# Normalising the residual sum of the MLP stage on ScalarE, with scale and bias per row from GpSimd, where VectorE subtracted and multiplied

## The chip, the cores and the metric

The kernel runs on one core of a Trainium2 chip. A core has TensorE (matmuls, PE in the profile; its weight loads are PEld), VectorE (DVE), ScalarE (ACT), GpSimd (POOL) and SyncE (SP), which here only issues transfers. The engines run side by side and are ordered by semaphores alone. The metric is the time of one execution on the device in microseconds; lower is better.

## The reference

The input `x` is 4096 tokens by 256. Three blocks follow each other, each with its own layernorm and residual sum:

```
x = x + 0.5 * ffn(layernorm(x))      # mixture of 8 experts (2 chosen) and a shared one
x = x + attn(layernorm(x))           # attention block with its own MLP, below
x = x + 0.5 * ffn(layernorm(x))

# inside attn, with z its input:
h = att @ Wo + bo + z
y = (h - mean(h)) * rsqrt(var(h) + 1e-5) * lnm_s + lnm_b
out = gelu(y @ W1 + b1) @ W2 + b2 + h
```

The change is in the line of `y`: the part `(h - mean) * rsqrt(var + eps)`. The factors `lnm_s` and `lnm_b` are folded into `W1` and `b1` when the stage starts.

## The kernel before

The program has four stages: `ffn_phase` (its names begin with `f_`), `attention_phase` (`a_`), `mlp_phase` (`m_`) and `ffn_phase` again (`g_`). Only `mlp_phase` is touched. It walks over the 4096 tokens in NB = 8 steps of 512, each held as NT = 4 tiles of 128 tokens by 256. Fp32 matmuls are made of three with split operands: for each operand ScalarE writes a rounded "hi" copy and VectorE the "lo" rest (`att_hi`/`att_lo`, `hT_hi`/`hT_lo`, `hid_hi`/`hid_lo`).

No scheduler sets the order. Each engine has a `body(i, par)`, written out by hand, and runs it for i = 0 to 8; steps 1 to 4 are turns of a loop. The order in one step i is:

- **TensorE**: first half of the projection of step i+1 (L1733), the second MLP matmul of step i-1 (`acc`, L1765), the transposes of `hn` (L1776, these wait for `hn` of step i), the second half of the projection of i+1, and the first MLP matmul (`hid`, L1789, which waits for `hT_lo`).
- **ScalarE**: four gelus and four `hid_hi` of step i-1, the first half of `att_hi` for step i+2 (L1561), two `hT_hi` (L1583), the second half of `att_hi`.
- **VectorE**: `h` (L1688), its statistics (L1691, L1696; mean and variance stand in `mv`), four `hid_lo` of step i-1 (L1658), the four rows of `hn` (L1707), the first half of `att_lo` for i+2 (L1653), two `hT_lo` (L1715), the second half of `att_lo`, and the result of step i-1 (L1724).
- **GpSimd**: `x_bias`, the second bias added to the residual input `xin` (four rows, L1621; it waits for the load of `xin`), then `rs = (var + eps)^-0.5` (L1638, L1640), then `xin += h` (L1643), then `z_bias` for step i+1, the first bias added to `zin` (four rows, L1621).
- **SyncE**: loads `zin` of i+1, two halves of the attention output of i+3 (L1504, each waits for the `att_lo` that frees its buffer), stores the result of i-1 (L1544, waits for L1724) and only then loads `xin` of i+1 (L1548).

So GpSimd's `rs`, and with it `hn`, stand behind the load of `xin`, and this load stands on SyncE's queue behind two halves of `att_lo` and the result of VectorE in the step before.

Of the kernel before, what the change touches and what calls it, by code (L numbers as in the profile page):

```python
# [23 lines left out]
ALU = mybir.AluOpType  # L24
ACT = mybir.ActivationFunctionType
AX = mybir.AxisListType

P = 128
# [7 lines left out]
DC = D // P  # L36
BT = 512
NT = BT // P
# [7 lines left out]
def stand_alone(eng, turns):  # L46


    eng.sem_inc(turns, 1)
# [1381 lines left out]
def mlp_phase(nc, turns, tag, w, att, z, x1, x2):  # L1431
# [9 lines left out]
    with ExitStack() as ctx:  # L1441
        m = Bank(nc, ctx, tag)
# [12 lines left out]
        mhalf = m.sb("mhalf", [P, NT])  # L1455
# [5 lines left out]
        h = m.sb("h", [P, NT, D])  # L1461
        st6 = m.sb("st6", [P, NT, 6])
        mv = m.sb("mv", [P, NT, 2])
        rs = m.sb("rs", [P, NT])
        hn = m.sb("hn", [P, NT, D])
        hT = m.sb("hT", [P, DC, 2, BT], F32R)
        act_out = m.sb("act_out", [P, HC, BT])
        hid_s = m.sb("hid_s", [P, HC, 2, BT], F32R)
        res = m.sb("res", [P, NT, D])
        proj = m.ps("proj", [P, NT, D])  # L1470
        hT_ps = m.ps("hT_ps", [P, DC, BT])
        hid = m.ps("hid", [P, 2, BT])
        acc = m.ps("acc", [P, NT, D])

        s = {n: m.sem(n) for n in (
            "w_in mhalf w1_scaled w_hi w_ready b1_ps att_in0 att_in1 att_hi att_lo z_in x_in zb x_b proj h bn stats "
            "veps rstd hn hT_ps hT_hi hT_lo hid gelu hid_hi hid_lo acc x_h res res_out").split()}
        NW = 8
        block = ctx.enter_context(nc.Block())

# [9 lines left out]
        def has(i, ahead=0):  # L1490

            return not isinstance(i, int) or 0 <= i + ahead < NB
# [59 lines left out]
        @block.scalar  # L1552
        def _(act):
            act.preload_act_table(ACT.Gelu_apprx_tanh)

            def att_hi(i, par, half):
                act.wait_ge(s["att_in%d" % half], i * 16 + 16)
                if has(i, -2):

                    act.wait_ge(s["proj"], i - 1)  # L1560
                act.activation(att_s[:, par, 0, half * HP:(half + 1) * HP], att_in[:, half],  # L1561
                               ACT.Identity).then_inc(s["att_hi"], 1)

            def gelu(i, hc):

                act.wait_ge(s["hid"], i * HC + hc + 1)
                act.activation(act_out[:, hc], hid[:, hc % 2], ACT.Gelu_apprx_tanh,
                               bias=b1[:, hc:hc + 1]).then_inc(s["gelu"], 1)

            def hid_hi(i, hc):  # L1570
                act.wait_ge(s["gelu"], i * HC + hc + 1)
                if has(i, -1):

                    act.wait_ge(s["acc"], i)
                act.activation(hid_s[:, hc, 0], act_out[:, hc], ACT.Identity).then_inc(s["hid_hi"], 1)

            def hT_hi(i):
                for c in range(DC):
                    act.wait_ge(s["hT_ps"], i * DC + c + 1)
                    if c == 0 and has(i, -1):  # L1580

                        act.wait_ge(s["hid"], i * HC)
                    act.activation(hT[:, c, 0], hT_ps[:, c], ACT.Identity).then_inc(s["hT_hi"], 1)  # L1583

            act.wait_ge(s["att_in0"], 16)
            act.activation(att_s[:, 0, 0, 0:HP], att_in[:, 0], ACT.Identity).then_inc(s["att_hi"], 1)
            act.wait_ge(s["att_in1"], 16)
            act.activation(att_s[:, 0, 0, HP:PAIRS], att_in[:, 1], ACT.Identity).then_inc(s["att_hi"], 1)
            act.wait_ge(s["w_in"], 16 * NW)
            act.activation(wo[:, 0], wo_in[:], ACT.Identity).then_inc(s["w_hi"], 1)  # L1590
            act.activation(w2[:, 0], w2_in[:], ACT.Identity).then_inc(s["w_hi"], 1)
            act.wait_ge(s["w1_scaled"], 1)
            act.activation(w1[:, 0], w1_in[:], ACT.Identity).then_inc(s["w_hi"], 1)
            for half in range(2):
                att_hi(1, 1, half)
            act.wait_ge(s["w_ready"], 3)

            def body(i, par):
                if has(i, -1):
                    gelu(i - 1, 0)  # L1600
                    for hc in range(1, HC):
                        gelu(i - 1, hc)
                        hid_hi(i - 1, hc - 1)
                    hid_hi(i - 1, HC - 1)
                if has(i, 2):
                    att_hi(i + 2, par, 0)
                if has(i):
                    hT_hi(i)
                if has(i, 2):
                    att_hi(i + 2, par, 1)  # L1610
            over_steps(act, body)

        @block.gpsimd
        def _(pool):
            pool.memset(mhalf[:], -0.5).then_inc(s["mhalf"], 1)
            pool.wait_ge(s["mhalf"], 1)
            pool.wait_ge(s["w_in"], 16 * NW)

            def add_rows(x, row):
                for t in range(NT):  # L1620
                    o = pool.tensor_tensor(x[:, t], x[:, t], row[:], ALU.add)  # L1621
                return o

            def z_bias(i, par):
                pool.wait_ge(s["z_in"], i * 16 + 16)
                add_rows(zin[:, par], bo).then_inc(s["zb"], 1)

            def x_bias(i, par):
                pool.wait_ge(s["x_in"], i * 16 + 16)
                add_rows(xin[:, par], b2).then_inc(s["x_b"], 1)  # L1630
            z_bias(0, 0)

            def body(i, par):
                if has(i):
                    x_bias(i, par)
                    pool.wait_ge(s["stats"], i + 1)
                    stand_alone(pool, turns)
                    pool.tensor_scalar(rs[:], mv[:, :, 1], EPS, None, ALU.add).then_inc(s["veps"], 1)  # L1638
                    pool.wait_ge(s["veps"], i + 1)
                    pool.tensor_tensor(rs[:], rs[:], mhalf[:], ALU.pow).then_inc(s["rstd"], 1)  # L1640

                    pool.wait_ge(s["x_b"], i + 1)
                    pool.tensor_tensor(xin[:, par], xin[:, par], h[:], ALU.add).then_inc(s["x_h"], 1)  # L1643
                if has(i, 1):
                    z_bias(i + 1, 1 - par)
            over_steps(pool, body)

        @block.vector
        def _(dve):
# [21 lines left out]
            for c in range(DC):  # L1671
                o = dve.tensor_scalar(w1_in[:, c], w1_in[:, c], ln[:, c, 0:1], None, ALU.mult)
# [8 lines left out]
            def body(i, par):  # L1681
                if has(i):
# [7 lines left out]
                    for t in range(NT):  # L1690
                        o = dve.bn_stats(st6[:, t], h[:, t])  # L1691
# [6 lines left out]
                if has(i, -1):  # L1698
                    for hc in range(HC):
                        hid_lo(i - 1, hc)  # L1700
                if has(i):
                    dve.wait_ge(s["rstd"], i + 1)
                    if has(i, -1):

                        dve.wait_ge(s["hT_ps"], i * DC)
                    for t in range(NT):
                        o = dve.tensor_scalar(hn[:, t], h[:, t], mv[:, t, 0:1], rs[:, t:t + 1],  # L1707
                                              ALU.subtract, ALU.mult)
                    o.then_inc(s["hn"], 1)
                if has(i, 2):  # L1710
                    att_lo(i + 2, par, 0)
                if has(i):
# [149 lines left out]
```

## Time and profile before

| | us |
|---|---|
| median of 3 runs | 2539.2 (2539.13 to 2540.71) |
| the profiled execution, whole | 2539.88 |
| its span in the profile | 2537.9 |
| busy PE / DVE / ACT / POOL | 2427.8 / 1911.5 / 1673.3 / 1496.3 |

The profile is of one execution. The rows of the trace give start and duration, in microseconds from the start of the span; the profiled execution is 1.98 us longer than its span. A row with `x4` merges four neighbouring instructions of a kind. The brackets at a row's end say how long the engine had been idle before it and what ended that. Ends of matmuls are modelled, so intervals between starts are safer on TensorE. The MLP stage takes its rows between about 2016 us, where its first loads are issued, and 2248 us.

### The profile page before, as it was taken

How to read it: one execution, taken by the hardware profiler on the slowest of the kernel's cores; microseconds unless marked ns; L12 is line 12 of the kernel's file. 1: busy time of each engine (PE TensorE's matmuls, PEld its weight loads, DVE VectorE, ACT ScalarE, POOL GpSimd, SP SyncE). 2: the span in 40 equal slices, each digit the busy share in tenths (PEclk: the TensorE clock that was granted, in tenths of full speed). 3: DMA queues.
4: the chain of work that ended last, by engine and by line, in shares of the span. 5: the costliest groups of instructions: out<-in, count | busy, mean ns of one | idle time of the engine just before them, and what ended most of it. 6: DMA issues, size and time to landing. Idle time of an engine off the chain costs nothing. (4 is left out here: it accounts for less than half of the span.)

```text
span 2537.9 us, 46611 instructions
## 1 busy us (share of the span) xinstructions
PE 2427.8 (96%) x14544; PEld 2107.4 (83%) x14544; DVE 1911.5 (75%) x3637; ACT 1673.3 (66%) x2887; POOL 1496.3 (59%) x1519
## 2 busy tenths in 40 slices
PE   7999899999999999999999999999999689959999
PEld 7888778888888888888888888888888589848888
DVE  4777677878878788787887878878788676736665
ACT  2455577878878777787877878878778533323333
POOL 2233377787677876878768777777776344412221
PEclk9999999999999999999999999999999899969999
DMA  3322531222212222122221222212221244321111
GB/s 131 142 99 91 176 115 42 84 77 81 92 42 83 80 77 92 42 83 83 75 91 42 83 83 75 91 42 88 78 75 51 87 164 153 100 89 34 50 50 42
DMA packets 128666, 212.73 MB, mean 84 GB/s; under 512 B 7652, under 2 KB 90776, under 8 KB 119960
## 3 DMA queue, kind: packets, MB, share of 16 engines
q1 hardware_dynamic: 128536, 211.36, 25.8%
q14 instruction: 93, 0.76, 0.1%
q8 instruction: 37, 0.61, 0.1%
HBM read 112.77 MB, written 48.23 MB: 63 GB/s over the span
## 5 line engine op out<-in xcount | busy, mean ns | idle before, releaser
L1295 DVE TENSOR_REDUCE a_nmax<-a_sc 128x1 f32<-128x1024 f32 x512 | 626.8, 1224 | 256.6 <-PE a_sc L1374 248.4
L1223 POOL TENSOR_SCALAR a_pr<-a_pr,a_rden 128x1024 f32<-128x1024 f32 x512 | 576.2, 1126 | 274.3 <-DVE a_rden L1300 204.0
L1147 ACT ACTIVATE a_pT<-a_tr 128x512 fp32r<-128x512 f32 x1024 | 559.9, 596 | 209.4 <-PE a_tr L1386 203.4
L1306 DVE TENSOR_TENSOR a_pT<-a_tr,a_pT 128x512 fp32r<-128x512 f32 x1024 | 650.4, 677 | 16.3 <-ACT a_pT L1147 16.3
L1410 PE MATMUL a_ov<-a_pT,a_v_s 128*128 128x512 f32 x2048 | 598.8, 414 | 2.4 <-DVE a_half L1286 1.4
L1153 ACT ACTIVATE a_pr<-a_sc,a_nmax 128x1024 f32<-128x1024 f32 x512 | 573.9, 1121 | 32.9 <-DVE a_nmax L1295 29.5
L1374 PE MATMUL a_sc<-a_k_s,a_q_s 128*128 128x512 f32 x2048 | 555.0, 393 | 8.1 <-DMA a_k_s<-a_k_s 7.8
L1386 PEld LDWEIGHTS a_tr<-f_ident,a_pr 128*128 128x128 f32 x4096 | 473.9, 140 | 91.5 <-DVE a_pT L1306 18.4
L1386 PE MATMUL a_tr<-f_ident,a_pr 128*128 128x128 f32 x4096 | 537.7, 273 | 8.6 <-DVE a_pT L1306 8.5
L1374 PEld LDWEIGHTS a_sc<-a_k_s,a_q_s 128*128 128x128 f32 x2048 | 380.9, 188 | 89.4 <-DMA a_k_s<-a_k_s 8.0
L1410 PEld LDWEIGHTS a_ov<-a_pT,a_v_s 128*128 128x128 f32 x2048 | 346.3, 189 | 53.2 <-issue 4.9
L1329 PE MATMUL a_pj<-a_z_s,a_wqk_s 128*128 128x512 f32 x756 | 193.8, 391 | 0.4 <-issue 0.4
L1329 PEld LDWEIGHTS a_pj<-a_z_s,a_wqk_s 128*128 128x128 f32 x756 | 141.7, 188 | 32.8 <-issue 0.8
L405 ACT ACTIVATE g_act_out<-g_hid,g_b 128x512 f32<-128x512 f32 x72 | 49.6, 688 | 154.2 <-PE g_hid L748 154.2
L1116 ACT ACTIVATE a_staged<-a_pj,f_bias 128x512 f32<-128x512 f32 x126 | 86.8, 689 | 88.7 <-PE a_pj L1329 66.4
L405 ACT ACTIVATE f_act_out<-f_hid,f_b 128x512 f32<-128x512 f32 x72 | 49.2, 684 | 118.3 <-PE f_hid L748 118.3
L782 PEld LDWEIGHTS f_acc<-f_w2p,f_hp 128*128 128x128 f32 x864 | 112.2, 190 | 9.3 <-DVE f_hp L591 4.5
L782 PEld LDWEIGHTS g_acc<-g_w2p,g_hp 128*128 128x128 f32 x864 | 112.5, 191 | 7.6 <-DVE g_hp L591 2.3
L782 PE MATMUL f_acc<-f_w2p,f_hp 128*128 128x256 f32 x864 | 115.9, 284 | 2.4 <-DVE f_hp L591 1.8
L748 PE MATMUL g_hid<-g_xT,g_w1p 128*128 128x512 f32 x432 | 116.9, 407 | 1.2 <-DVE g_w1p L643 1.2
L782 PE MATMUL g_acc<-g_w2p,g_hp 128*128 128x256 f32 x864 | 115.8, 284 | 0.9 <-DVE g_hp L591 0.4
L748 PE MATMUL f_hid<-f_xT,f_w1p 128*128 128x512 f32 x432 | 115.5, 403 | 0.0
(221 smaller groups left out, 3216.6 us busy)
## 6 DMA issues: line engine op xcount, KB each, us to landing
a_z_s<-zT SPq DMA_DIRECT2D x32, 1024.0 KB, 7.4
a_k_s<-a_k_s SPq DMA_DIRECT2D x64, 512.0 KB, 5.6
a_wqk_s<-w_split SPq DMA_DIRECT2D x64, 256.0 KB, 3.1
a_v_s<-a_v_b SPq DMA_DIRECT2D x16, 1024.0 KB, 4.6
att<-a_ao SPq DMA_DIRECT2D x32, 512.0 KB, 2.9
m_att_in<-att SPq DMA_DIRECT2D x16, 1024.0 KB, 5.4
a_wv_s<-w_split SPq DMA_DIRECT2D x17, 512.0 KB, 3.8
zT<-f_zT SPq DMA_DIRECT2D x8, 1024.0 KB, 3.9
```

The source lines that it names most:

```text
L405: act.activation(act_out[:, e % 3], hid[:, (par + e) % 2], ACT.Gelu, bias=b1[:, weights_of(e):weights_of(e) + 1]).then_inc(s["gelu"], 1)
L748: o = pe.matmul(hid[:, (par + e) % 2], w1p[:, a, (c * NE + x) * HID:(c * NE + x + 1) * HID], xT[:, par, c, b], start=(n == 0), stop=(n == 5))
L782: o = pe.matmul(acc[:, t], hp[:, e % 3, a, t * P:(t + 1) * P], w2p[:, b, x * D:(x + 1) * D], start=False, stop=(e == NE - 1 and (a, b) == ...
L1147: act.activation(pT[:, (u // 4) % 2, 0, 4 * part:4 * part + 4, (u % 4) * P:(u % 4 + 1) * P], tr[:, part].rearrange("p (t q) -> p t q", t=4 ...
L1153: act.activation(pr[:, k % NP], sc[:, k % 2], ACT.Exp, bias=nmax[:, k % NP:k % NP + 1], accum_out=den[:, k % NP:k % NP + 1]).then_inc(s["e ...
L1223: pool.tensor_scalar(pr[:, k % NP], pr[:, k % NP], rden[:, k % NP:k % NP + 1], 1.0, ALU.mult, ALU.mult).then_inc(s["normed"], 1)
L1295: dve.tensor_reduce(nmax[:, k % NP:k % NP + 1], sc[:, k % 2], AX.X, ALU.max, negate=True).then_inc(s["negmax"], 1)
L1306: dve.tensor_tensor(to[:, 1], tr[:, part].rearrange("p (t q) -> p t q", t=4), to[:, 0].bitcast(F32), ALU.subtract).then_inc(s["tr_lo"], 1)
L1329: o = pe.matmul(bank[:], wqk_s[:, "QK".index(kind), c, a], z_s[:, c * 2 + b, part], start=(i == 0), stop=(i == 5))
L1374: o = pe.matmul(sc[:, k % 2, kb * BT:(kb + 1) * BT], q_s[:, slot, head, tile * P:(tile + 1) * P], k_s[:, slot, head, a, kb * BT:(kb + 1) * ...
L1386: o = pe.transpose(tr[:, part, j * P:(j + 1) * P], pr[:, (k - LAG) % NP, (4 * part + j) * P:(4 * part + j + 1) * P], ident[:])
L1410: o = pe.matmul(ov[:], v_s[:, vslot, kt, 2 * vhead:2 * vhead + 2] .rearrange("p k f -> p (k f)"), pT[:, blk % 2, a, kt], start=(kt == 0 an ...
```

## The change

ScalarE works out `hn = h * rs + shift` with `rs` as scale and `shift = -mean * rs` as bias, both one value for each partition. GpSimd works out `shift` in two more instructions of 128x4: `-mean` ahead of the `rs` steps, and the product behind the power. The signal on which `hn` waits (`rstd`) now comes from the product; the power signals `powed`. ScalarE does `hn` behind the `hid_hi` of step i-1 and ahead of the first half of `att_hi`. VectorE's four instructions go.

```
@@ ScalarE, body(i, par)
                     hid_hi(i - 1, HC - 1)
+                if has(i):
+                    act.wait_ge(s["rstd"], i + 1)
+                    if has(i, -1):
+                        act.wait_ge(s["hT_ps"], i * DC)
+                    for t in range(NT):
+                        o = act.activation(hn[:, t], h[:, t], ACT.Identity, bias=shift[:, t:t + 1], scale=rs[:, t:t + 1])
+                    o.then_inc(s["hn"], 1)
                 if has(i, 2):
                     att_hi(i + 2, par, 0)
@@ GpSimd, body(i, par)
                     pool.wait_ge(s["stats"], i + 1)
+                    if has(i, -1):
+                        pool.wait_ge(s["hn"], i)
                     stand_alone(pool, turns)
+                    pool.tensor_scalar(shift[:], mv[:, :, 0], -1.0, 0.0, ALU.mult, ALU.add)
                     pool.tensor_scalar(rs[:], mv[:, :, 1], EPS, None, ALU.add).then_inc(s["veps"], 1)
                     pool.wait_ge(s["veps"], i + 1)
-                    pool.tensor_tensor(rs[:], rs[:], mhalf[:], ALU.pow).then_inc(s["rstd"], 1)
+                    pool.tensor_tensor(rs[:], rs[:], mhalf[:], ALU.pow).then_inc(s["powed"], 1)
+                    pool.wait_ge(s["powed"], i + 1)
+                    pool.tensor_tensor(shift[:], shift[:], rs[:], ALU.mult).then_inc(s["rstd"], 1)
@@ VectorE, body(i, par)
-                if has(i):
-                    dve.wait_ge(s["rstd"], i + 1)
-                    if has(i, -1):
-                        dve.wait_ge(s["hT_ps"], i * DC)
-                    for t in range(NT):
-                        o = dve.tensor_scalar(hn[:, t], h[:, t], mv[:, t, 0:1], rs[:, t:t + 1],
-                                              ALU.subtract, ALU.mult)
-                    o.then_inc(s["hn"], 1)
                 if has(i, 2):
                     att_lo(i + 2, par, 0)
```

ScalarE's order in a turn of the loop, before, from the last `hid_hi` on (`m_att_s` is written by `att_hi`, `m_hT` by `hT_hi`):

```order
L1575 ACTIVATE m_hid_s<-m_act_out 128x512 x2
L1557 ISA
L1561 ACTIVATE m_att_s<-m_att_in 128x2048
L1579 ISA
L1582 REGISTER_ALU
L1583 ACTIVATE m_hT<-m_hT_ps 128x512
```

The same place of ScalarE's order after the change (`m_hn` is the normalised sum, `m_shift` and `m_rs` its bias and scale):

```order
L1576 ACTIVATE m_hid_s<-m_act_out 128x512 x2
L1610 REGISTER_ALU
L1612 ACTIVATE m_hn<-m_h,m_shift,m_rs 128x256 x4
L1558 ISA
L1562 ACTIVATE m_att_s<-m_att_in 128x2048
L1580 REGISTER_ALU
```

The four rows of `hn` now stand ahead of the first half of `att_hi`, which used to run while ScalarE had nothing else to do.

GpSimd's order in a turn of the loop, before:

```order
L1621 TENSOR_TENSOR m_xin<-m_xin,m_b 128x256 x4
L1636 REGISTER_ALU
L1638 TENSOR_SCALAR m_rs<-m_mv 128x4
L1640 TENSOR_TENSOR m_rs<-m_rs,m_mhalf 128x4
L1643 TENSOR_TENSOR m_xin<-m_xin,m_h 128x1024
```

GpSimd's order at this place after the change:

```order
L1630 TENSOR_TENSOR m_xin<-m_xin,m_b 128x256 x4
L1645 REGISTER_ALU
L1649 TENSOR_SCALAR m_shift<-m_mv 128x4
L1650 TENSOR_SCALAR m_rs<-m_mv 128x4
L1652 TENSOR_TENSOR m_rs<-m_rs,m_mhalf 128x4
L1654 TENSOR_TENSOR m_shift<-m_shift,m_rs 128x4
L1657 TENSOR_TENSOR m_xin<-m_xin,m_h 128x1024
```

Two small instructions are added, one ahead of the old pair and one behind it; the large sum `xin += h` and `z_bias` follow as before.

## Rows read from the trace of the kernel before

**Rows 1.** Busy time by stage (us from:to, length, engines, clock, DMA).

```profile
2052.00:2217.00 165.00, 160.41 (x1184) 151.49 (x1184) 119.15 (x158) 61.11 (x79) 67.59 (x77) 1.00 0.40 129
```

**Rows 2.** TensorE's waits in the MLP stage: us in total, times, longest.

```profile
PE m_acc L1765 <- DVE m_hid_s L1658: 5.2, 2, 2.6
PE m_hT_ps L1776 <- DVE m_hn L1707: 3.6, 5, 2.2
```

**Rows 3.** TensorE in order of time (start, us), steps 0, 1, 2 and 5.

```profile
2052.95 5.93 PE L1733 MATMUL m_proj<-m_wo,m_att_s 128*128 128x256 f32 x48 [1.41 <-DVE m_h L1688]
2061.10 1.09 PE L1776 MATMUL m_hT_ps<-m_ident,m_hn 128*128 128x128 f32 x8 [2.21 <-DVE m_hn L1707]
...
2079.00 5.84 PE L1765 MATMUL m_acc<-m_w,m_hid_s 128*128 128x256 f32 x48
2084.68 1.03 PE L1776 MATMUL m_hT_ps<-m_ident,m_hn 128*128 128x128 f32 x8
...
2102.59 5.84 PE L1765 MATMUL m_acc<-m_w,m_hid_s 128*128 128x256 f32 x48
2108.75 1.09 PE L1776 MATMUL m_hT_ps<-m_ident,m_hn 128*128 128x128 f32 x8 [0.32 <-DVE m_hn L1707]
...
2181.11 1.09 PE L1776 MATMUL m_hT_ps<-m_ident,m_hn 128*128 128x128 f32 x8 [0.33 <-DVE m_hn L1707]
```

**Rows 4.** All other engines in step 2, from one `xin` load to the next.

```profile
2092.48 0.43 SPq L1548 DMA_DIRECT2D m_xin<-x  x1
...
2099.80 2.81 POOL L1621 TENSOR_TENSOR m_xin<-m_xin,m_b 128x256 f32<-128x256 f32 x4 [15.49 <-DMA m_xin<-x]
...
2102.58 0.23 POOL L1638 TENSOR_SCALAR m_rs<-m_mv 128x4 f32<-128x4 f32 x1
...
2103.90 2.40 POOL L1643 TENSOR_TENSOR m_xin<-m_xin,m_h 128x1024 f32<-128x1024 f32 x1
2104.06 4.63 DVE L1707 TENSOR_SCALAR m_hn<-m_h,m_mv,m_rs 128x256 f32<-128x256 f32 x4 [4.43 <-POOL m_rs L1640]
2106.26 3.03 POOL L1621 TENSOR_TENSOR m_zin<-m_zin,m_bo 128x256 f32<-128x256 f32 x4
2108.61 2.82 DVE L1653 TENSOR_TENSOR m_att_s<-m_att_in,m_att_s 128x2048 fp32r<-128x2048 f32 x1
...
2109.52 1.09 ACT L1583 ACTIVATE m_hT<-m_hT_ps 128x512 fp32r<-128x512 f32 x2 [8.89 <-PE m_hT_ps L1776]
...
2110.49 1.92 ACT L1561 ACTIVATE m_att_s<-m_att_in 128x2048 fp32r<-128x2048 f32 x1
...
2112.55 2.27 DVE L1653 TENSOR_TENSOR m_att_s<-m_att_in,m_att_s 128x2048 fp32r<-128x2048 f32 x1
...
2116.62 0.46 SPq L1548 DMA_DIRECT2D m_xin<-x  x1
```

**Rows 5.** GpSimd in step 1.

```profile
2073.85 3.79 POOL L1621 TENSOR_TENSOR m_xin<-m_xin,m_b 128x256 f32<-128x256 f32 x4 [12.22 <-DMA m_xin<-x]
2077.61 0.23 POOL L1638 TENSOR_SCALAR m_rs<-m_mv 128x4 f32<-128x4 f32 x1
```

**Rows 6.** GpSimd in step 5.

```profile
2174.94 0.23 POOL L1638 TENSOR_SCALAR m_rs<-m_mv 128x4 f32<-128x4 f32 x1
```

**Rows 7.** First stage: GpSimd's four small steps, and ScalarE behind them.

```profile
154.92 0.19 POOL L452 TENSOR_SCALAR f_zshift<-f_zmv 128x4 f32<-128x4 f32 x1 [9.20 <-DVE f_zmv L496]
...
156.91 2.08 ACT L350 ACTIVATE f_zz<-f_res,f_zshift,f_zrs 128x256 f32<-128x256 f32 x4 [0.23 <-POOL f_zshift L465]
```

**Rows 8.** Durations (ns, least/median/most) of ScalarE's normalising rows in the first stage.

```profile
L350 ACT ACTIVATE f_zz<-f_res,f_zshift,f_zrs x32: 584/587/604, 92.2 to 327.7; 128x256 f32<-128x256 f32 x32
```

**Rows 9.** The same for VectorE's `hn` rows in the MLP stage.

```profile
L1707 DVE TENSOR_SCALAR m_hn<-m_h,m_mv,m_rs x32: 401/828/2482, 2056.4 to 2222.6; 128x256 f32<-128x256 f32 x32
```

**Rows 10.** VectorE's normalising rows in the last stage, GpSimd idle.

```profile
2259.26 1.38 DVE L509 TENSOR_SCALAR g_xn<-g_xin,g_mv,g_rs 128x256 f32<-128x256 f32 x4 [1.57 <-POOL g_rs L455]
```

**Rows 11.** TensorE in step 7, in order of time.

```profile
2219.71 7.46 PE L1765 MATMUL m_acc<-m_w,m_hid_s 128*128 128x256 f32 x48 [2.62 <-DVE m_hid_s L1658]
```

**Rows 12.** Busy time by stretch, step 7: the third number from the end is TensorE's clock.

```profile
2220.00:2224.00 4.00, 4.00 (x23) 4.00 (x23) 3.01 (x4) 0.00 (x0) 1.89 (x1) 0.57 0.00 0
```

More of the change, by code:

```diff
@@ L1464, in mlp_phase @@
         rs = m.sb("rs", [P, NT])
+        shift = m.sb("shift", [P, NT])
         hn = m.sb("hn", [P, NT, D])
@@ L1476, in mlp_phase @@
             "w_in mhalf w1_scaled w_hi w_ready b1_ps att_in0 att_in1 att_hi att_lo z_in x_in zb x_b proj h bn stats "
-            "veps rstd hn hT_ps hT_hi hT_lo hid gelu hid_hi hid_lo acc x_h res res_out").split()}
+            "veps powed rstd hn hT_ps hT_hi hT_lo hid gelu hid_hi hid_lo acc x_h res res_out").split()}
         NW = 8
```

## Prediction

> **What bounds the kernel now.** I read the table of stages first: in the 165 us of the MLP stage between its start-up and its last step TensorE is busy for 160.4 us at full clock [rows 1]. At first sight nothing that VectorE does there can be worth much: what is to be had is the time in which TensorE waits. The list of waits names it: TensorE waits for `hn` five times, 3.6 us together and 2.2 us at the longest, and twice for `hid_lo`, which the change doesn't touch [rows 2]. In order of time the first is step 0 (2.21 us), step 1 has none, and steps 2 to 5 have 0.3 to 0.5 us each [rows 3].
>
> The waits understate the delay, since ends of matmuls are modelled; starts are safer. In step 1, where there is no wait, the transposes start 2084.68 - 2079.00 = 5.68 us after the 48 matmuls ahead of them. In step 2 it is 6.16 us, a delay of 0.48 where the bracket says 0.32; in step 0 it is 2061.10 - 2052.95 = 8.15 us, a delay of 2.47 [rows 3]. Steps 3 to 5 hold the rest of the 3.6 us, 3.6 - 2.2 - 0.3 = 1.1, and with 0.16 more for each 1.6. In sum `hn` holds TensorE up by 2.5 + 0.5 + 1.6 = 4.5 us. That is all that an earlier `hn` can give back.
>
> The question is why `hn` is late in steps 2 to 5. Following step 2 back through the engines gives a ring [rows 4]. The load of `xin` is issued at 2092.48, lands 7.3 us later, GpSimd adds the bias for 2.8 us, and at T = 2102.58 begins the variance steps. `hn` starts on VectorE at T+1.5 and ends at T+6.1; `att_lo` follows at T+6.0 and ends at T+8.85; then VectorE is busy without a gap (two `hT_lo`, the second `att_lo`, the result) until SyncE issues the next `xin` load at 2116.62, T+14.0. The turn takes 24.14 us. TensorE's own step, from 2079.00 to 2102.59 where nothing held it, takes 23.59 [rows 3]. So the stage runs at the pace of this ring, half a microsecond a step slower than TensorE, although TensorE looks full. An edit that only brought `hn` forward, and left the ring as long, would win a fixed time once and not one for every step.
>
> **The change part by part.**
>
> *GpSimd's two small instructions.* They and their waits can be read in the first stage, which has the same four steps: from the start of the first to ScalarE's start it is 156.91 - 154.92 = 1.99 us [rows 7], against 2104.06 - 2102.58 = 1.48 here [rows 4]. So `hn` starts 0.51 us later. `xin += h` and `z_bias`, behind them in GpSimd's queue, are later by about as much.
>
> *The four rows of `hn`.* On VectorE they take 4.63 us [rows 4], the single ones 401 to 2482 ns with a median of 828 [rows 9]: an instruction that takes 0.35 us where GpSimd is idle (1.38 for four [rows 10]) is stretched where GpSimd's sums run beside it, as `xin += h` and `z_bias` do from 2103.90 to 2109.29 [rows 4]. On ScalarE four rows of this very form take 2.08 us [rows 7], and 32 of them lie between 584 and 604 ns [rows 8], so nothing there stretches them. `hn` ends at T + 1.99 + 2.08 = T+4.07 in place of T+6.1, 2.0 us earlier. The bounds of this term: 4 x 0.604 = 2.4 us above, 2.1 below.
>
> The Trainium skill ("ScalarE: Activation LUTs", section "Rules for kernel authors") speaks against this edit: for add and mul use VectorE, not ScalarE. With VectorE alone the trace agrees, 1.38 against 2.08 us, and by the rule `hn` would come 0.70 + 0.51 = 1.2 us later, about 1.2 us of loss in each of five steps that wait, 6 us in all. At this place the trace doesn't agree, since what is replaced is 4.63 us.
>
> *ScalarE's queue.* `hn` stands ahead of the first half of `att_hi` (1.92 us). ScalarE had been idle for 8.89 us ahead of `hT_hi` [rows 4], and 2.08 + 1.92 have room there. But `att_hi`, done long before until now, can only begin when `hn` ends: it ends at T + 4.07 + 1.92 = T+6.0. `att_lo` waits for it and is ready to start at T+6.0, where it started before at T+6.03. So this wait takes the place of the work that went, and VectorE's 4.6 us are not taken out of the ring at all: they turn into idle time. `hT_hi` behind it is free at T+6.0, when the transposes are just being done. No cost there.
>
> *`att_lo` beside `z_bias`.* GpSimd's product ends near T+1.9, `xin += h` takes 2.40 to T+4.3, and four rows of `z_bias` at 0.70 (a quarter of 2.81) start at T+4.3, 5.0, 5.7 and 6.4 [rows 4]. In the rows of before VectorE gets its turn when a row of GpSimd ends. So `att_lo`, ready at 6.0, runs from 6.4 for 2.27 us to T+8.67, against T+8.85. The ring gets shorter by 0.2 us and takes 23.96. If it has to let the last row pass too, it ends at 7.1 + 2.27 = T+9.4, and the ring gets longer by 0.5; if it never waits, T+8.3, shorter by 0.55. I take -0.2, from the rule of turns.
>
> *Steps 0 and 1.* In step 0 TensorE's transposes come 2.0 us earlier (of 2.47) and everything on TensorE behind them too. The next `xin` load doesn't: it hangs on `att_lo`. But its bias rows in step 1 took 3.79 us and not 2.81, beside the `hid_lo` rows [rows 4, 5]; `hid_lo` follows TensorE and is over earlier, and of that 1.0 us I take 0.7. In step 1 the ring went at TensorE's pace: the `xin` load was issued 2092.48 - 2077.61 = 14.87 us after T and not 14.0 [rows 4, 5], since the transposes came late for it. That 0.8 goes too.
>
> *The sum.* T of step 2 comes earlier by 0.7 + 0.8 + 0.2 = 1.7, and with 0.2 from each of three more turns T of step 5 by 2.3: 2174.94 - 2.3 = 2172.6 [rows 6], and `hn` ends at 2176.7. TensorE running freely from step 0 on would be there 2.0 + 0.5 + 1.6 = 4.1 us earlier than now, at 2177.0 against 2181.11 [rows 3]. The two all but meet, `hn` just ahead: TensorE should wait no more after step 0, and the gain is 4.1 us. Behind step 5 nothing is touched: in step 7 TensorE waits for `hid_lo`, and that chain starts from its own matmuls. Both bounds together: 4.5 us at the most, and with the ring longer by 0.5 a turn and nothing from the bias rows T of step 5 is later by 4 x 0.5 - 0.8 = 1.2, `hn` ends at 2180.2, and the gain is 0.9.
>
> Against its own time the profiled execution goes from 2539.88 to 2535.8; the median of the runs lies 0.7 below it, so 2539.2 - 4.1 = 2535.1 us.
>
> **The rivals.** What can be told from no change here is about 0.2%, 5.1 us on either side. The forecast is inside it.
>
> *The ring still sets the pace.* If it keeps its 24.1 us and only steps 0 and 1 give something, T of step 5 is earlier by 1.5, less 0.5 if `att_lo` lets one more row pass in some turns; `hn` ends at 2178.0, and the gain is 3.1 at the most and 0.9 by the bound above, in the middle 2.0 us: 2537.2. For it speaks that the two pass each other with only 0.3 us between them; against it that `att_lo` leads the queue at a row's end.
>
> *The clock at the end of the stage.* In step 7 TensorE stood idle for 2.62 us, then the granted clock was 0.57 for 4 us, between its two levels of 1.2 and 2.4 GHz, and 48 matmuls took 7.46 us where the same ones take 5.84 [rows 3, 11, 12]. If the shift by 4 us moves this stretch off the matmuls, 1.6 us more are won: 2533.5, and with as much again at the start of the next stage 2531.9, faster by more than 0.2%. It can as well cost as much: 2536.7. Nothing in the rows says which way.
>
> *Slower: `hn` on ScalarE stretched as on VectorE.* If GpSimd's sums held ScalarE's rows up too and they took 4.6 us, `att_hi` would end at T + 1.99 + 4.6 + 1.9 = T+8.5 and `att_lo` at T+10.8, 1.95 us later than now in every turn. Over five turns T of step 5 is 9.8 later, `hn` another 0.5: 2549.5, slower. The point from which this decides is about 2.6 us for the four rows: with x us each turn grows by x - 2.3 and `hn` itself shifts by x - 4.1, and 5(x - 2.3) + x - 4.1 passes zero there. Against it stand 32 rows within 20 ns [rows 8].
>
> *The change doesn't do what it says.* `hn` would still come last, behind a late `rs`: then TensorE's waits for `hn` stay, and with the fixed gain of step 0 alone it is 2537.1. This falls together with the first rival.
>
> **How the numbers follow.** TensorE free after step 0: 0.60, 2535.1. The ring still in force: 0.20, 2537.2. The clock at the end helps by more than a microsecond: 0.14, 2532 to 2533.5. Slower by the stretched `hn`: 0.03, and 0.03 for a clock that costs twice as much. The range from 2532.0 to 2538.3 takes in the gain of 0.9, the whole 4.5, and the clock to both sides, and leaves out less than 2 in 10. Faster by over 0.2% (under 2534.1): 0.17; within: 0.80; slower (over 2544.3): 0.03.
>
> **What the profile after will show.** Right: `hn` rows on ScalarE at about 0.52 us each behind one another, starting 2.0 us after GpSimd's first small step; no wait of TensorE for `hn` beyond step 0, about 0.2 us by its bracket there; VectorE idle ahead of `att_lo`, released by `att_hi`; steps of 23.6 us between starts of `acc`; 160 us of TensorE's work in a stretch shorter by 4. Wrong: waits of TensorE for `hn` in steps 3 to 5 (the ring holds, its turn over 24.0), `hn` rows over 0.65 us, `att_lo` that starts later than T+6.5, `xin` landing more than 7.5 us after its issue, or a difference that lies outside the MLP stage.

## The result, and the profile after

| | before | after |
|---|---|---|
| median of 7 runs each | 2539.18 us | 2531.02 us |
| lowest to highest | 2537.87 to 2541.38 | 2529.70 to 2532.12 |
| ratio, with 95% interval | | 0.9967 [0.9955, 0.9978] |
| profiled execution / its span | 2539.88 / 2537.9 | 2530.85 / 2529.1 |
| busy PE / DVE / ACT / POOL | 2427.8 / 1911.5 / 1673.3 / 1496.3 | 2421.5 / 1870.3 / 1690.6 / 1511.2 |

The change gains 8.2 us where 4.1 were forecast, and the median lies 1 us below the range. In the profiles all of it has come up by TensorE's first work of the last stage: the projection of step 1 starts 0.84 us later than before, that first work (L715) 8.98 us earlier (2260.79 and 2251.81).

The same TensorE rows as [rows 3, 11], after (start, duration, idle time before it and what ended it):

```profile
2053.79 5.93 PE L1738 MATMUL m_proj<-m_wo,m_att_s 128*128 128x256 f32 x48 [1.41 <-DVE m_h L1702]
2059.95 1.09 PE L1781 MATMUL m_hT_ps<-m_ident,m_hn 128*128 128x128 f32 x8 [0.23 <-ACT m_hn L1612]
...
2077.84 5.62 PE L1770 MATMUL m_acc<-m_w,m_hid_s 128*128 128x256 f32 x48
2083.30 1.04 PE L1781 MATMUL m_hT_ps<-m_ident,m_hn 128*128 128x128 f32 x8
...
2101.14 5.62 PE L1770 MATMUL m_acc<-m_w,m_hid_s 128*128 128x256 f32 x48
2106.60 1.04 PE L1781 MATMUL m_hT_ps<-m_ident,m_hn 128*128 128x128 f32 x8
...
2177.80 1.09 PE L1781 MATMUL m_hT_ps<-m_ident,m_hn 128*128 128x128 f32 x8 [0.21 <-ACT m_hn L1612]
...
2216.08 5.72 PE L1770 MATMUL m_acc<-m_w,m_hid_s 128*128 128x256 f32 x48 [2.62 <-DVE m_hid_s L1672]
...
2232.66 5.73 PE L1770 MATMUL m_acc<-m_w,m_hid_s 128*128 128x256 f32 x48 [2.62 <-DVE m_hid_s L1672]
```

Before, the last of these (step 8) read:

```profile
2238.09 8.71 PE L1765 MATMUL m_acc<-m_w,m_hid_s 128*128 128x256 f32 x48 [2.62 <-DVE m_hid_s L1658]
```

Counted from the projection of step 1, the transposes of step 0 come 1.99 us earlier and those of step 5, at 2177.80 for 2181.11, 3.31 + 0.84 = 4.15 us: there the forecast of 4.1 is met. Then three things stand in the rows that it did not have. The 48 `acc` matmuls of steps 7 and 8 take 5.7 us each, not 7.46 and 8.71: 4.7 us more, 0.4 of it by the second point. And a step that nothing holds up takes 2101.14 - 2077.84 = 23.30 us, not 23.59; `acc` itself takes 5.62 for 5.84.

The third stands where the last stage begins. Its first load, and VectorE's first row on what was loaded, before and then after:

```profile
2251.43 0.38 SPq L238 DMA_DIRECT2D g_xin<-x  x1
2255.75 1.41 DVE L491 BATCH_NORM_STATS2 g_st<-g_xin 128x6 f32<-128x256 f32 x4 [7.69 <-DMA g_xin<-x]
```

```profile
2243.04 0.38 SPq L238 DMA_DIRECT2D g_xin<-x  x1
2246.78 1.41 DVE L491 BATCH_NORM_STATS2 g_st<-g_xin 128x6 f32<-128x256 f32 x4 [7.13 <-DMA g_xin<-x]
```

From the issue to VectorE's row it is 4.32 us before and 3.74 after. This is no scatter: it is 4.25 to 4.36 us in the profiles of all six kernels whose `hn` is on VectorE, and 3.74 to 3.82 in all eight with `hn` on ScalarE. So about 0.5 us of the gain lies behind the stage, where the prediction had "nothing is touched". Why is not shown.

Where the other 4.3 us come from, stretches of before (PE busy and the count of its matmuls come first, the clock third from the end):

```profile
2236.00:2240.00 4.00, 1.91 (x9) 1.91 (x10) 1.34 (x3) 1.23 (x3) 0.00 (x0) 0.69 0.02 4
2240.00:2244.00 4.00, 4.00 (x20) 4.00 (x20) 0.00 (x0) 0.00 (x0) 0.00 (x0) 0.50 0.00 0
```

And of after, around `acc` of step 7 and behind that of step 8:

```profile
2216.00:2220.00 4.00, 3.92 (x34) 3.92 (x35) 0.03 (x1) 2.08 (x4) 2.43 (x2) 1.00 0.00 0
2220.00:2224.00 4.00, 2.68 (x24) 2.44 (x23) 1.09 (x2) 1.09 (x2) 0.00 (x0) 1.00 0.00 0
...
2240.00:2244.00 4.00, 0.00 (x0) 0.00 (x0) 0.00 (x0) 0.95 (x1) 0.90 (x5) 0.76 0.38 131
```

TensorE did the same in both: it stood idle for 2.62 us, then began 48 matmuls. Before, the granted clock went to its lower level (1.2 GHz) for some microseconds about when they began, both times; after, it stayed at 2.4 GHz until the stage was over.

TensorE's waits after, to be read beside [rows 2]:

```profile
PE m_acc L1770 <- DVE m_hid_s L1672: 5.2, 2, 2.6
PE m_hid L1794 <- DVE m_hT L1720: 1.6, 1, 1.6
PE m_proj L1738 <- DVE m_h L1702: 1.4, 1, 1.4
PE m_hT_ps L1781 <- ACT m_hn L1612: 0.9, 4, 0.3
```

`hn` is still waited for four times (steps 0, 3, 4 and 5). Step 2 of the ring after, as [rows 4] show it before:

```profile
2091.38 0.43 SPq L1549 DMA_DIRECT2D m_xin<-x  x1
...
2099.34 2.82 POOL L1630 TENSOR_TENSOR m_xin<-m_xin,m_b 128x256 f32<-128x256 f32 x4 [12.61 <-DMA m_xin<-x]
2102.24 0.20 POOL L1649 TENSOR_SCALAR m_shift<-m_mv 128x4 f32<-128x4 f32 x1
...
2104.25 2.08 ACT L1612 ACTIVATE m_hn<-m_h,m_shift,m_rs 128x256 f32<-128x256 f32 x4 [6.87 <-POOL m_shift L1654]
2106.23 1.90 ACT L1562 ACTIVATE m_att_s<-m_att_in 128x2048 fp32r<-128x2048 f32 x1
2106.45 4.87 POOL L1630 TENSOR_TENSOR m_zin<-m_zin,m_bo 128x256 f32<-128x256 f32 x4
...
2108.17 2.55 DVE L1667 TENSOR_TENSOR m_att_s<-m_att_in,m_att_s 128x2048 fp32r<-128x2048 f32 x1 [9.99 <-ACT m_att_s L1562]
...
2115.91 0.46 SPq L1549 DMA_DIRECT2D m_xin<-x  x1
...
2126.03 0.19 POOL L1649 TENSOR_SCALAR m_shift<-m_mv 128x4 f32<-128x4 f32 x1
```

`hn` starts 2.01 us after GpSimd's first small step and takes 2.08 us; `att_hi` ends at T + 5.89, `att_lo` runs from T + 5.93 to T + 8.48. VectorE is idle for 9.99 us ahead of it. A turn takes 2126.03 - 2102.24 = 23.79 us. The ring is as it was forecast.

### The profile page after: what moved, and what is told of

Its sections match the earlier page's. It is cut to its first block and busy times, and to the rows that moved or that the text cites. A ratio compares the mean times of both kernels' runs of the same rounds, so it can differ in the third digit from the quotient of the medians.

```text
span 2529.1 us, 46630 instructions
## 1 busy us (share of the span) xinstructions
PE 2421.5 (96%) x14544; PEld 2102.1 (83%) x14544; DVE 1870.3 (74%) x3605; ACT 1690.6 (67%) x2919; POOL 1511.2 (60%) x1535
```

## Experiments

Each kernel was timed in five rounds against the kernel before on its chip, whose median there was 2540.17 (before_pad, after_shift_last, both "late"), 2540.16 (pool_part, after_att_first, both "rs_first") or 2541.19 (the last four). "Full clock" is the mean of a kernel's runs of (time - (1 - granted clock) x span): what is left when the time lost to the lower clock is taken off. It is an estimate: the clock of a run is given to 0.001, which is 2.5 us. Yet with the estimate the scatter of the old kernel's 65 runs falls from 2.6 to 1.4 us (standard deviation). The third column compares medians; the means can differ from it by up to 1.2 us, and the ratio lies nearer to them (before_fill: -4.08 by the medians, -3.4 by the means).

| kernel | median | against before, same chip | ratio [95%] | mean clock | full clock |
|---|---|---|---|---|---|
| before (three sets, 65 runs) | 2540.2 to 2541.2 | | | 0.9833 to 0.9836 | 2498.2 to 2498.8 |
| the change | 2531.02 | -8.16 | 0.9967 [0.9955, 0.9978] | 0.9846 | 2492.0 |
| before_pad | 2540.24 | +0.07 | 1.0000 [0.9991, 1.0009] | 0.9835 | 2498.5 |
| after_shift_last | 2531.97 | -8.20 | 0.9959 [0.9945, 0.9972] | 0.9850 | 2493.6 |
| before_late | 2542.48 | +2.31 | 1.0005 [0.9996, 1.0015] | 0.9831 | 2499.1 |
| after_late | 2533.15 | -7.02 | 0.9966 [0.9954, 0.9978] | 0.9843 | 2493.4 |
| pool_part | 2539.40 | -0.76 | 0.9998 [0.9989, 1.0006] | 0.9847 | 2501.2 |
| after_att_first | 2535.64 | -4.52 | 0.9982 [0.9972, 0.9991] | 0.9845 | 2496.7 |
| before_rs_first | 2534.62 | -5.54 | 0.9979 [0.9968, 0.9990] | 0.9838 | 2494.5 |
| after_rs_first | 2531.30 | -8.86 | 0.9963 [0.9950, 0.9977] | 0.9847 | 2492.0 |
| before_fill | 2537.11 | -4.08 | 0.9987 [0.9979, 0.9996] | 0.9852 | 2499.9 |
| after_fill | 2529.71 | -11.48 | 0.9955 [0.9942, 0.9968] | 0.9858 | 2493.5 |
| after_rs_fill | 2527.64 | -13.55 | 0.9950 [0.9937, 0.9963] | 0.9858 | 2492.6 |
| after_again (the change once more) | 2532.51 | -8.68 | 0.9970 [0.9958, 0.9982] | 0.9840 | 2492.2 |

### Why the matmuls are faster: where the tiles lie

The new tile `shift` has 16 bytes in each partition and is allocated between `rs` and `hn`. It moves `hn`, `hT`, `act_out`, `hid_s` and `res`, from 32 bytes behind a multiple of 64 onto one if every size is rounded up to 32 bytes (worked out from the sizes of the allocations; no profile shows an address). Two kernels take this apart: before_pad has the shift of addresses and nothing else, after_shift_last the change without it.

```
before_pad:        rs = m.sb("rs", [P, NT])
                  +pad = m.sb("pad", [P, NT])          # never used
after_shift_last: -shift = m.sb("shift", [P, NT])      # between rs and hn
                   res = m.sb("res", [P, NT, D])
                  +shift = m.sb("shift", [P, NT])
```

> The kernel before with one unused tile of 16 bytes per partition allocated between rs and hn, so that hn, hT, act_out, hid_s and res lie where they lie after the change; no instruction differs. Theory P (addresses): the starts of the acc matmuls come 113 to 114 ns apart and not 118, those of hid 231 and not 233, so a step in which TensorE waits for nothing takes 23.3 us in place of 23.6. Steps 2 to 5 are held by the ring and gain nothing; steps 1 and 6 to 8 gain 0.2 to 0.3 us each: about -1.2 us by itself, 2538.0, and more or less by whatever TensorE's clock does in steps 7 and 8 (up to -4.6). Rival (something else in the change, such as VectorE's missing rows, speeds the matmuls up): 118 ns and 2539.2 as before.

> The changed kernel with the tile shift allocated behind res, so that hn, hT, act_out, hid_s and res lie where they lay before the change; no instruction differs. Theory P (addresses): acc matmuls 118 ns apart again, free steps of 23.6 us, and since the ring takes about 23.8 us TensorE hardly waits for hn in steps 3 to 5: about +1.2 us, 2532.2, with the clock of steps 7 and 8 as it happens to fall (up to +4.6 more). Rival: 113 ns stay and the time stays at 2531.0.

The `acc` matmuls of one stretch (start 2078.8 to 2082), their least, median and longest ns, in the order before, the change, before_pad, after_shift_last:

```profile
L1765 PE MATMUL m_acc<-m_w,m_hid_s x26: 277/280/285, 2079.0 to 2082.0; 128*128 128x256 f32 x26
```

```profile
L1770 PE MATMUL m_acc<-m_w,m_hid_s x29: 276/276/276, 2078.8 to 2081.9; 128*128 128x256 f32 x29
```

```profile
L1766 PE MATMUL m_acc<-m_w,m_hid_s x28: 276/276/276, 2078.8 to 2081.9; 128*128 128x256 f32 x28
```

```profile
L1770 PE MATMUL m_acc<-m_w,m_hid_s x28: 277/280/285, 2078.8 to 2081.9; 128*128 128x256 f32 x28
```

The pace follows the place of the tiles and nothing else in the change: with the empty tile the old kernel has it, and without it the new one loses it. From start to start the matmuls are 113.5 ns apart instead of 118 (48 of them from 2077.84 to 2083.30 after, from 2079.00 to 2084.68 before).

The old kernel gains nothing by it: +0.07 us, where 1.2 were expected. Its steps 2 to 5 are held by the ring and stay at 24.1 to 24.3 us, and TensorE's waits for `hn` grow from 3.6 to 4.8. What the other steps save is lost again in its profile ahead of `acc` of step 7, where TensorE stands idle for 4.77 us instead of 2.62: the last two rows of `hid_lo`, which take 1.29 us before, now meet GpSimd's small steps and its large sum.

```profile
2217.68 3.44 DVE L1659 TENSOR_TENSOR m_hid_s<-m_act_out,m_hid_s 128x512 fp32r<-128x512 f32 x2 [0.68 <-ACT m_hid_s L1576]
2217.87 2.70 POOL L1644 TENSOR_TENSOR m_xin<-m_xin,m_h 128x1024 f32<-128x1024 f32 x1
```

In the changed kernel the addresses are worth 2493.6 - 2492.0 = 1.6 us at full clock. The medians don't show it (-8.20 for -8.16 against before). The rows do: after_shift_last, with what the clock took in steps 7 and 8 left out, is 0.4 us longer than the change from the transposes of step 0 to those of step 5, 0.3 from there to `acc` of step 7, and 0.6 from there to the last stage, 1.3 us in all.

### Whether the moment decides on the clock

Both kernels once more, with 1.75 us of work on VectorE ahead of the stage's first `wo` rest, so that all that follows comes later; nothing else is altered. Two theories were at issue: C, that the moment at which TensorE's idle time falls decides whether the clock drops, and D, that something else does, the code that runs there or VectorE's `hn` rows beside TensorE, so that the old kernel keeps its slow rows and the changed one has none.

```
+dve.tensor_tensor(<act_out, 128x1536>, <wo_in>, <wo_in>, ALU.add)   # result never read
```

> The kernel before with one more VectorE sum of 128x1536 (about 1.75 us, its result is not used) ahead of the lo part of Wo, so that all work of the MLP stage comes 1.75 us later. Theory C (the clock falls in steps 7 and 8 by the moment at which TensorE's idle times of 2.6 us come, and a shift of everything moves it): the rows of acc in steps 7 and 8, 7.46 and 8.71 us before, change, by up to -4.6 us together; the time is anywhere from 2536.3 to 2541.0, and the difference from 2541.0 is what these rows and the start of the last stage show. Rival D (the fall belongs to the code that runs there, not to the moment): 7.46 and 8.71 us stay and the time is 2539.2 + 1.75 = 2541.0.

> The changed kernel with the same extra VectorE sum of about 1.75 us ahead of the lo part of Wo. Theory C (moment): acc of steps 7 and 8, 5.7 us each after the change, can take 7.5 or more again: 2532.8 to 2537.4. Rival D (VectorE's hn rows beside TensorE make the clock fall, and they are gone): both rows stay at 5.7 us and the time is 2531.0 + 1.75 = 2532.8.

The changed kernel, delayed:

```profile
2215.51 7.33 PE L1771 MATMUL m_acc<-m_w,m_hid_s 128*128 128x256 f32 x48 [2.62 <-DVE m_hid_s L1672]
...
2233.70 5.73 PE L1771 MATMUL m_acc<-m_w,m_hid_s 128*128 128x256 f32 x48 [2.62 <-DVE m_hid_s L1672]
```

```profile
2216.00:2220.00 4.00, 4.00 (x26) 4.00 (x26) 0.00 (x0) 1.62 (x4) 1.85 (x1) 0.67 0.00 0
```

D has fallen: the changed kernel, with no `hn` rows on VectorE, has the slow matmuls of step 7 back, 7.33 us, with a clock of 0.67, and the old one, delayed, has 7.46 and 5.94 us for 7.46 and 8.71. The times alone would not have told: by the medians the delayed kernels are 2.3 us slower than the old one on the same chip and 2.1 us slower than the change, near the 1.8 us that D had for both.

C isn't shown by this either. The change itself, run again without the delay (below), has slow rows in both steps, so it needs no delay to bring them back. What the clock takes in steps 7 and 8 is the matter of a run; what decides is open. In the profiles of the five old kernels without the filling that is tried below the two rows together take 0 to 4.3 us more than undisturbed, in those of the six new ones 0 to 3.3 us. So the 4.3 us of the profiled pair are the end of this scatter, not a property of the change.

### GpSimd's part alone

The two small instructions on GpSimd stay, `hn` stays on VectorE, `shift` is allocated behind `res` and never read.

```
+pool.tensor_scalar(shift[:], mv[:, :, 0], -1.0, 0.0, ALU.mult, ALU.add)
 pool.tensor_scalar(rs[:], mv[:, :, 1], EPS, None, ALU.add) ...
 pool.tensor_tensor(rs[:], rs[:], mhalf[:], ALU.pow) ...
+pool.tensor_tensor(shift[:], shift[:], rs[:], ALU.mult) ...
```

> The kernel before with GpSimd's two added steps alone: hn still on VectorE, but behind the product, and shift is allocated behind res, so addresses stay. Theory R: hn starts 0.5 us later in every turn and the ring grows from 24.1 to 24.6: TensorE's waits for hn grow by 0.5 us in step 0 and by 0.5 in each of steps 2 to 5, and step 1 gets a small one: +2.5 us, 2541.7, aside from the clock in steps 7 and 8. Rival (the added steps hide behind the other work of GpSimd): 2539.2 to 2539.7.

TensorE's wait in it:

```profile
PE m_hT_ps L1780 <- DVE m_hn L1711: 6.6, 5, 2.7
```

Steps 2 to 5 grow to 24.6 to 24.9 us and the wait from 3.6 to 6.6 us: the later start costs in every turn, 0.57 to 0.65 us for the 0.51 forecast. A delay that met no ring would cost once. At full clock it loses 3.0 us (2501.2 against 2498.2), near the 2.5 expected. The median shows nothing of it (-0.76), since its runs had a higher clock, 0.9847 for 0.9833. Taken as time alone, this experiment would have misled.

### `att_hi` ahead of `hn`

The changed kernel, ScalarE's first half of `att_hi` put ahead of `hn` again, where it used to stand. The theory: `att_lo` need not wait for `hn` any more, and the ring gets shorter.

```
+if has(i, 2):
+    att_hi(i + 2, par, 0)
 if has(i):
     ...                    # the four rows of hn
-if has(i, 2):
-    att_hi(i + 2, par, 0)
```

> The changed kernel with ScalarE's first half of att_hi ahead of the four hn rows again, as in the kernel before. Theory R (the pace of steps 3 to 5 is set by the ring xin load, x_bias, rs, hn, att_hi, att_lo, result, xin load): hn and att_hi leave the ring, att_lo runs long before, a turn falls below TensorE's 23.3 us, TensorE waits for hn in step 0 alone, and three steps of 23.7 to 23.8 us become 23.3: -1.3 us, 2529.7, aside from the clock in steps 7 and 8. Rival (the waits of 0.2 to 0.3 us are only those of hn's own latency): the three waits stay and so does 2531.0.

A clear miss: 4.6 us slower than the change (4.7 at full clock), where 1.3 faster was expected. GpSimd and VectorE in it, step 3, and TensorE's wait:

```profile
2127.95 4.87 POOL L1630 TENSOR_TENSOR m_xin<-m_xin,m_b 128x256 f32<-128x256 f32 x4 [12.24 <-DMA m_xin<-x]
2128.83 2.70 DVE L1667 TENSOR_TENSOR m_att_s<-m_att_in,m_att_s 128x2048 fp32r<-128x2048 f32 x1 [1.03 <-ACT m_att_s L1562]
```

```profile
PE m_hT_ps L1781 <- ACT m_hn L1614: 4.7, 5, 2.0
```

`att_lo` is early indeed, and for that it now runs beside `x_bias`, which takes 4.87 us for 2.82. `x_bias` stands ahead of `rs`, so `hn` is 2 us late and TensorE waits 4.7 us in all. The Trainium skill ("SBUF — State Buffer", "Who interferes with whom") says that a VectorE instruction with two SBUF inputs contends with a GpSimd instruction that reads SBUF, and that the ports they share are an exclusive lock. This trace agrees: GpSimd's four rows grow by 2.05 us beside one VectorE sum, which itself takes 2.70 us for 2.27, and `z_bias` in the change grows by the same amount (4.87). So the wait of `att_lo` for `hn`, which came with the change, does good: it moves the collision from rows that `rs` waits for to rows that nothing waits for.

### Taking the ring apart

The theory says that `hn` is late because `rs` stands behind the `xin` load. Without this order there is no ring through `hn`. GpSimd works out `rs` first and adds the bias afterwards:

```
-x_bias(i, par)
 ...                        # rs (and shift)
+x_bias(i, par)
 pool.wait_ge(s["x_b"], i + 1)
 pool.tensor_tensor(xin[:, par], xin[:, par], h[:], ALU.add)
```

> The kernel before with GpSimd's two steps for rs ahead of x_bias, so that they don't wait for the load of xin. VectorE still works out hn. Theory R: the load leaves the chain to hn, hn is done several us before TensorE needs it from step 1 on, TensorE's delays of steps 2 to 5 (2.06 us by starts) go, the delay of 2.47 us in step 0 stays or falls where GpSimd's sums no longer run beside it: 2537.1, aside from the clock in steps 7 and 8, which can take or give up to 4.6. Rival (not the ring but GpSimd's sums beside the hn rows): steps 2 to 5 still wait and the time is within 0.5 us of 2539.2.

> The changed kernel with GpSimd's small steps ahead of x_bias. Theory R: no wait of TensorE for hn beyond step 0, steps of 23.3 us throughout: -1.3 us, 2529.7, aside from the clock in steps 7 and 8. Rival: as it is, 2531.0.

TensorE in the old kernel with this order:

```profile
2102.45 5.84 PE L1765 MATMUL m_acc<-m_w,m_hid_s 128*128 128x256 f32 x48
...
2126.04 5.84 PE L1765 MATMUL m_acc<-m_w,m_hid_s 128*128 128x256 f32 x48
...
2149.63 5.84 PE L1765 MATMUL m_acc<-m_w,m_hid_s 128*128 128x256 f32 x48
```

```profile
PE m_hT_ps L1776 <- DVE m_hn L1707: 0.6, 1, 0.6
```

With `hn` still on VectorE, five waits become one of 0.6 us, the steps fall to 23.59, and 5.5 us are gained, 3.7 to 4.3 at full clock (2494.5 against 2498.2 to 2498.8). By the rows it is 3.7: 2.06 in steps 2 to 5, as expected, and 1.62 in step 0, which the expectation had left open (2537.1 without it). It needs neither ScalarE nor `shift`.

One thing more differs here. In step 2 `hn` starts 4.66 us earlier (2099.40), and its four rows also take 2.65 us for 4.63, since they run beside `x_bias` and no longer beside `xin += h`. So this run alone would not tell the place of `rs` from the stretched rows. The others do: in pool_part the rows stand where they stood, and a later `rs` makes every turn longer; in the change `hn` is not stretched at all, and TensorE still waits in steps 3 to 5 until `rs` leaves the ring. In the changed kernel the same order makes all steps 23.29 us, as expected, but of the 1.3 us forecast nothing can be told: -8.86 for -8.16 against before, 2492.0 at full clock in both. The profile shows where half of the 1.3 us saved on the waits goes: TensorE idles 3.38 us ahead of `acc` of step 7 instead of 2.62.

### Keeping the clock up

If what the clock takes is set off by TensorE's idle time, matmuls without use in it should give it back. Both kernels get 20 of them ahead of `acc` in step 7, 12 ahead of `hid` there and 20 ahead of `acc` in step 8, where `proj` isn't used any more.

```
+def fill(n):
+    pe.wait_ge(s["h"], NB)
+    for _ in range(n):
+        pe.matmul(proj[:, 0], wo[:, 0, 0, 0:P], wo[:, 0, 0], start=True, stop=True, ...)
+if isinstance(i, int) and i >= NB - 1:
+    fill(20)
 pe.wait_ge(s["hid_lo"], i * HC)
+if isinstance(i, int) and i == NB - 1:
+    fill(12)
 pe.wait_ge(s["hT_lo"], i * DC + DC)
```

> The kernel before with matmuls whose result is not used in TensorE's idle times of steps 7 and 8 (20 ahead of each of the two late acc groups, 12 ahead of the last hid group, into the PSUM of proj, which is free by then), so that TensorE doesn't stand idle inside the stage. Theory C (the idle times of 2.6 us let the clock fall or not, by the moment): the clock stays at its upper level through steps 7 and 8, acc takes 5.7 us in both, which saves about 2 us on average over runs and up to 4.6 in one: mean 2538.2. Rival (the clock falls for another reason than idle time): rows of 7 us and more come back, and the mean stays at 2540.4.

> The changed kernel with the same filling matmuls. Theory C: against before_fill the tail no longer plays a part, and what is left is the change's own work: 4.2 us from earlier hn, and 1.5 us from matmuls that read hid_s and hT at the new addresses, 5.7 us below before_fill: mean 2532.5 if before_fill is 2538.2. That is not below the changed kernel's 2531.0, whose profile had no fall in the tail at all. Rival (the change lowers the time by 8 to 9 us without the clock): 8 us or more below before_fill.

> The changed kernel with GpSimd's small steps ahead of x_bias and with the filling matmuls, a candidate for the fastest version. Ring theory: no wait for hn beyond step 0 and no fall of the clock in steps 7 and 8: 0.9 us below after_fill. Rival: as after_fill.

> The changed kernel itself, beside the kernel before on one chip. Theory C: single runs of both kernels scatter with the share of time at the lower clock; the mean clock of before is lower (0.9833 to 0.9836 in 48 runs against 0.9846 in 7), and with more runs part of this gap closes: mean 2531 to 2533, 7.5 to 9 us below before. Rival (the gap in the clock was chance): mean 2534, 6 us below.

The old kernel with the filling, the same stretches as above and in [rows 12]:

```profile
2220.00:2224.00 4.00, 3.46 (x29) 3.46 (x30) 1.78 (x5) 0.00 (x0) 0.00 (x0) 1.00 0.00 0
2236.00:2240.00 4.00, 3.77 (x31) 3.56 (x31) 1.29 (x2) 0.57 (x2) 0.00 (x0) 1.00 0.00 0
2240.00:2244.00 4.00, 3.38 (x29) 3.18 (x27) 0.59 (x1) 0.00 (x0) 0.00 (x0) 1.00 0.00 0
```

The clock no longer falls there. In the eleven profiles without filling it fell at 10 of the 22 idle times ahead of `acc` of steps 7 and 8, in the three with filling at none of six. The old kernel is 4.1 us faster (3.4 by the means; 2.2 were expected) by matmuls that compute nothing: the mean clock goes from 0.9834 to 0.9852, worth 4.6 us of a span of 2537, and 1.1 us are paid at full clock (2499.9 for 2498.8). In the new kernel the filling brings 2.8 us (2529.71 for 2532.51 on the same chip; 3.4 by the means). With the new order on GpSimd as well (after_rs_fill) the median is 2527.64, 13.6 us below before and the lowest of all, 4.9 us below the change run beside it. Against after_fill it is 2.1 us by the medians and 0.9 by the means, where 0.9 was expected; with five runs each this isn't told from nothing.

The change run again is the answer to how much of its first profile was luck:

```profile
2214.59 7.41 PE L1770 MATMUL m_acc<-m_w,m_hid_s 128*128 128x256 f32 x48 [2.62 <-DVE m_hid_s L1672]
...
2232.85 7.32 PE L1770 MATMUL m_acc<-m_w,m_hid_s 128*128 128x256 f32 x48 [2.62 <-DVE m_hid_s L1672]
```

Here the clock fell in both steps, and the rows take 3.3 us more than in the first profile; yet the gain over before stands, 8.7 us (8.1 by the means, where 7.5 to 9 were expected). With the filling in both kernels, where steps 7 and 8 run at 2.4 GHz, the change is worth 7.4 us by the medians (8.0 by the means) and 6.4 at full clock. The theory had 5.7 and its rival 8 or more, so the medians lie between the two and this doesn't decide.

## Why the prediction was wrong

**What held.** The term of `hn`: 2.08 us on ScalarE, started 2.01 us after GpSimd's first step (1.99 forecast). The ring as what sets the pace, with `att_hi` in the place of the work that went: a turn of 23.96 was forecast, 23.79 and 23.90 measured, since VectorE started `att_lo` at T + 5.93 without waiting for a row's end; it lost 0.28 us within it (2.55 for 2.27). The gain in step 0 (2.0 forecast, 1.99) and up to step 5 (4.1 forecast, 4.15). The price of GpSimd's part: taken as a delay of every turn, and 3.0 us when run alone.

**The step that failed first: what TensorE's own step takes.** The forecast of 4.1 us is met at step 5, but not by its own term alone: 3.7 of it are `hn`'s and 0.4 the addresses'. The sum took 23.59 us from the rows of before as a constant. The change adds a tile, and no step of the working asked where this puts the others. It made the free step 23.30, 1.6 us in all at full clock. The forecast that TensorE waits no more after step 0 failed by the same: the ring's 23.8 to 23.9 us would nearly have vanished behind 23.6, and against 23.3 it shows, with 0.2 to 0.3 us in each of steps 3 to 5. It is the first rival in form, but with the ring 0.2 to 0.3 us shorter than that rival had it. In after_shift_last, which has the old pace, the steps held up by the ring are no more than 0.2 us over 23.59.

**The step that failed second: the size of the clock.** The rival "the clock at the end of the stage" had the right place and mechanism and too small a price. It took 1.6 us from step 7, doubled it as a guess and had 0.14 + 0.03 for it. Step 8, with the same idle time of 2.62 us ahead of it, has no place in the working; its row of 8.71 us holds 2.8 more than the undisturbed 5.94. It was also wrong to treat it as one event that goes one way. It differs from run to run: the 65 runs of before lie between 2535.2 and 2545.9 us, and their means by granted clock are 2544.5 (0.982), 2541.4 (0.983), 2538.8 (0.984), 2537.9 (0.985). The three runs shown, within 1.6 us of each other, hid this.

**A third, smaller: "behind step 5 nothing is touched".** About 0.5 us come from the earlier start of VectorE on the first load of the last stage, and about 0.9 of the 1.3 us of the addresses lie behind step 5.

**The sum as it is now.** Of the 8.2 to 8.7 us, 6.0 to 6.8 are work at full clock (2498.2 to 2498.8 less 2492.0 or 2492.2). The rows divide the 4.15 of them that are there by step 5: from the transposes of step 0 to those of step 5 it is 120.01 us before, 117.85 after, and without the addresses, in after_shift_last, 118.27:

```profile
2058.72 1.09 PE L1781 MATMUL m_hT_ps<-m_ident,m_hn 128*128 128x128 f32 x8 [0.23 <-ACT m_hn L1612]
...
2176.99 1.09 PE L1781 MATMUL m_hT_ps<-m_ident,m_hn 128*128 128x128 f32 x8
```

So 0.4 of them are the addresses' and 3.7 are `hn`'s, of the 4.5 that its waits held. Over the whole stage, up to TensorE's first work of the last one, the rows give 3.7 us from `hn`, 1.3 from the addresses and 0.5 from the first load of the last stage, 5.5 in all; the other 4.3 of the 9.8 between the two profiles are the clock's. At full clock the change without the addresses gains 4.6 to 5.2, and the addresses 1.4 to 1.6; these differences are sure to about 1 us. The remaining 2 us or so of the medians are the clock: mean 0.9840 to 0.9846 for 0.9833 to 0.9836.

**What stays open.** Why the mean clock is higher after the change. The profiles show that the same idle time is followed by a fall of the clock in one execution and not in another; they don't show what decides, nor why the new kernel should fare better on average, and with 13 runs of it against 65 it may be less than it looks. It isn't steps 7 and 8 alone: with both filled the kernels still differ by 7.4 us in the median against 6.4 at full clock. The profiles also have other falls that vary by run, one of 3.4 us near 382 us and one at the start of the MLP stage, which no experiment touched. Nor was it tried which of the five moved tiles makes the matmuls faster (`hid_s`, which all `acc` matmuls load, is the nearest guess), or any other address than these two. And it is open why VectorE's first row of the last stage comes 0.5 us earlier behind its load.

## What to carry over

Ask of every new tile, however small, which other tiles it moves, and test it alone with an empty one: here 16 bytes were worth a fifth of the gain, and showed only once the ring was out of the way. Where a ring sets the pace, look for what is in it only by order: `rs` ahead of `x_bias` brings most of the gain with no change of engines (3.7 to 4.3 of 6.0 to 6.8 us at full clock). And before sizing an effect of some microseconds, read the clock of every stretch that follows an idle time of TensorE, and compare at full clock: pool_part lost 3 us of work and looked like no change.

## What the runs showed of the hardware

- Fp32 matmuls of 128x128 by 256 columns, made of split operands, are 113.5 ns apart or 118 ns, by where their SBUF operands lie: a 16-byte tile allocated ahead of them switches it, in the old kernel and in the new. By the sizes of the allocations the faster place is a multiple of 64 bytes and the slower one 32 bytes off it. The first projection, whose tiles didn't move, kept 5.93 us for 48.
- Idle gaps of TensorE of 2.6 us and more ahead of 48 matmuls were followed by 0 to 2.8 us lost in these; in one program by nothing twice in one execution (after) and by 1.7 and 1.6 us in another (after_again). Useless matmuls in three gaps made the old kernel 4.1 us faster by the medians and 3.4 by the means, of 2541 (ratio 0.9987 [0.9979, 0.9996]).
- Four GpSimd rows of 128x256 take 2.82 us alone and 4.87 beside one VectorE sum of 128x2048. Four normalising rows of 128x256 take 1.38 us on VectorE with GpSimd idle and 4.63 beside GpSimd's sums. On ScalarE they take 2.08 us, 585 to 605 ns each, with GpSimd's sum of 128x1024 beside them.
